# An adaLN-FFN kernel on one core: weight scales repeated by transfers instead of TensorE, the first convolution evicted by ScalarE, and a new order in front of the loop

## What is computed

```python
...
        out = lax.conv_general_dilated(x, weight, window_strides=(STRIDE,), padding=[(PAD, PAD)], dimension_numbers=('NCH', 'OIH', 'NCH'), feature_group_count=GROUPS)
        ctx = jnp.einsum('nd,od->no', c, c_weight)
        out = out + ctx[:, :, None] + bias[None, :, None]
...
        w_scale = jnp.max(jnp.abs(weight), axis=-1, keepdims=True) / QMAX
        w_q = jnp.round(weight / w_scale).astype(jnp.int8)
        a_scale = jnp.max(jnp.abs(input_act), axis=-1, keepdims=True) / QMAX
        x_q = jnp.round(input_act / a_scale).astype(jnp.int8)
        acc = jnp.matmul(x_q.astype(jnp.int32), w_q.T.astype(jnp.int32))
        scale = a_scale * w_scale.T[None, :, :]
        out = (acc.astype(jnp.float32) * scale).astype(jnp.float16)
...
    x = x + _L0_ffn_ref(_L0_cond_ref(x, cond_128, L0_cond_weight, L0_cond_c_weight, fside_S_0), L0_ffn_weight)
    x = x + _L1_ffn_ref(_L1_cond_ref(x, cond_128, L1_cond_W0, L1_cond_b0, L1_cond_W1, L1_cond_b1, L1_cond_W2, L1_cond_b2, L1_cond_weight, L1_cond_bias_k), L1_ffn_W, L1_ffn_b, L1_ffn_A, L1_ffn_Bmat, L1_ffn_LiMEs)
```

## Time and profile before

| | |
|---|---|
| runs | 612.49, 613.61, 615.41 us; median 613.61 |
| the profiled execution's own time | 613.3 us |
| its span (first to last instruction) | 611.5 us |
| granted TensorE clock | 0.999 of full speed |
| busy: PE, DVE, ACT, POOL | 604.1, 433.3, 357.0, 375.0 us |
| transfers | 136.24 MB, mean 223 GB/s |

### The profile page before, as it was taken

How to read it: one execution, slowest core, us unless ns; L and a number is a source line. 1 busy time by engine, 2 the same in 40 slices (tenths; PEclk the granted TensorE clock), 3 DMA queues, 4 the chain that set the end, 5 groups by cost and what they waited for, 6 DMA issues and landing times.

```text
span 611.5 us, 16208 instructions
## 1 busy us (share of the span) xinstructions
PE 604.1 (99%) x6500; PEld 343.7 (56%) x6500; DVE 433.3 (71%) x883; ACT 357.0 (58%) x622; POOL 375.0 (61%) x252
## 2 busy tenths in 40 slices
PE   8999999999999999999999999999999999999998
PEld 5756667667776777765554444444444444444444
DVE  5988999978899999986877757754635454355543
ACT  3799998989999999876535234453233333321100
POOL 3436545546777666554888945989777659656200
PEclk9999999999999999999999999999999999999999
DMA  8989987878889999684183125765445445542111
GB/s 338 357 268 311 366 317 277 295 261 307 318 315 333 323 336 312 232 293 140 66 305 116 34 71 201 284 234 192 159 172 185 153 169 216 207 147 94 70 69 70
DMA packets 38632, 136.24 MB, mean 223 GB/s; under 512 B 5036, under 2 KB 5580, under 8 KB 38513
## 3 DMA queue, kind: packets, MB, share of 16 engines
q1 hardware_dynamic: 33518, 118.43, 54.6%
q10 hardware_dynamic: 5040, 16.78, 6.8%
HBM read 87.95 MB, written 47.24 MB: 221 GB/s over the span
## 4 chain that ended last, share of the span: by engine, by line
PE 87%; DVE 1%; issue 1%; ACT 0%; DVEq 0%
PE ps L908 42%; PE ps L612 16%; PE ps L517 9%; PE ps L709 7%; PE ps L596 4%; PE ps L890 2%; PE ps L581 2%; PE ps L657 2%; PE ps L652 1%; PE ps L621 1%; PE ps L625 0%; PE ps L692 0%; DVE yb L1459 0%; PE ps L677 0%; ACT zT L1096 0%
## 5 line engine op out<-in xcount | busy, mean ns | idle before, releaser
L612 PE MATMUL ps<-wqT,yq_both 128*128 128x512 bf16 x512 | 122.4, 379 | 0.3 <-DVE yb L1459 0.3
L1284 POOL TENSOR_TENSOR x<-x_in,f_all 128x512 f32<-128x512 f32 x64 | 74.3, 1162 | 51.1 <-DVE f_all L1496 51.0
L1288 POOL TENSOR_TENSOR x_split<-x_ph,x_split 128x1032 f16<-128x1032 f32 x25 | 53.7, 2148 | 55.5 <-ACT x_split L994 55.5
L1021 ACT ACTIVATE yv<-yb,yinv 128x128 f32<-128x128 f32 x256 | 77.8, 388 | 0.0
L1323 POOL TENSOR_TENSOR ring<-ring 128x512 f32<-128x512 f32 x56 | 72.8, 1300 | 4.3
L612 PEld LDWEIGHTS ps<-wqT,yq_both 128*128 128x128 bf16 x512 | 45.5, 99 | 46.3 <-issue 1.4
L517 PE MATMUL ps<-x_split,conv_h 128*64 128x256 f16 (+1 forms) x1248 | 60.0, 275 | 0.0
L1496 DVE SCALAR_TENSOR_TENSOR f_all<-ps,tok_scale,wsc_b 128x512 f16<-128x512 f32 x64 | 47.9, 749 | 16.7 <-PE ps L612 15.6
L517 PEld LDWEIGHTS ps<-x_split,conv_h 128*64 128x64 f16 (+1 forms) x1248 | 47.5, 108 | 9.7 <-issue 7.9
L1817 DVE SCALAR_TENSOR_TENSOR x_in<-ps,unscale,x_in 128x512 f32<-128x512 f32 x30 | 22.5, 750 | 39.9 <-PE ps L908 39.9
L1817 DVE SCALAR_TENSOR_TENSOR wst<-ps,unscale,wst 128x512 f32<-128x512 f32 x27 | 20.2, 750 | 36.7 <-PE ps L908 36.7
(11 more groups left out here) (351 smaller groups left out, 1321.5 us busy)
## 6 DMA issues: line engine op xcount, KB each, us to landing
x_in<-in_x SPq DMA_DIRECT2D x32, 512.0 KB, 6.0
x_scratch<-x SPq DMA_DIRECT2D x32, 512.0 KB, 3.7
x_ph<-in_x_phases SPq DMA_DIRECT2D x31, 516.0 KB, 5.2
x_scratch<-ring SPq DMA_DIRECT2D x26, 512.0 KB, 5.0
ring<-x_scratch SPq DMA_DIRECT2D x26, 512.0 KB, 5.2
x_in<-x_scratch SPq DMA_DIRECT2D x12, 512.0 KB, 3.5
out<-x_in ACTq DMA_DIRECT2D x12, 512.0 KB, 3.5
wst<-in_w_rows SPq DMA_DIRECT2D x10, 512.0 KB, 6.7
```

Of the source, the lines that this page charges most:

```text
L612: last = mm(acc_bank(t, h), yqT[:, t % 2, p, :], wqT[:, p, h * HALF:(h + 1) * HALF], start=p == 0, stop=p == PH - 1)
L1021: last = A(yv[:, s, :], yb[:, t % 2, s, :], ACT.Copy, scale=yinv[:, s:s + 1], bias=MAGIC)
L1284: g.tensor_tensor(x1[:, t % 2, s], x_in[:, t % 3, s], f16[:, s], ALU.add).then_inc(sem("x1_ready"), 1)
L1288: g.tensor_tensor(x_split[:, (t - SPLIT) % 2, 1, :], phases(t), x_split[:, (t - SPLIT) % 2, 0, :], ALU.subtract).then_inc(sem("xl_ready"), 1)
```

## The change

- The matmuls that spread the scales are gone, and so are both copies to `wsc_b`. Instead ScalarE issues, per half, a transfer that writes four columns of `wq_scale` to a scratch in DRAM (`save_scales`, 128 x 4 floats, each of them by itself since the DRAM side is transposed), waits for it, and issues one that reads 512 scales back to all 128 partitions (`load_scales`). `layer0(0, h)` waits for the second. What TensorE had waited for ahead of those matmuls (`agg_ready`, `agg_b_ready`, `limesT_ready`) it now waits for at `int_product(0, h)`.
- The bias and eviction of convolution 0 go from VectorE (one instruction of 1024 columns) to ScalarE (`first_bias`, eight of 128 columns).
- What stands in front of the loop is in a new order on SP, PE, ACT and DVE. Loop step 3 is written out ahead of the loop and woven into the rest; the loop starts at 4.

```diff
+        scales_dram = nc.dram_tensor("scales_scratch", [L], F32, kind="Internal").ap()
...
             load_phases(0)
             sp.dma_start(conv_w[:, :, :], conv_taps).then_inc(sem("conv_w_loaded"), 16)
             load_wq(1)
-            sp.dma_start(pk[:, PACK_1:PACK_W], pack[:, PACK_1:PACK_W]).then_inc(sem("pack2_loaded"), 16)
+            sp.dma_start(kw, mix_rows).then_inc(sem("kw_loaded"), 16)
             load_wq(2)
-            sp.dma_start(kw, mix_rows).then_inc(sem("kw_loaded"), 16)
             load_phases(1)
             load_wq(3)
             load_wq(4)
-            load_phases(2)
             load_wq(5)
             load_wq(6)
+            sp.dma_start(pk[:, PACK_1:PACK_W], pack[:, PACK_1:PACK_W]).then_inc(sem("pack2_loaded"), 16)
+            load_phases(2)
+            load_phases(3)
+            load_phases(SPLIT)
             load_wq(7)
+            load_x(0)
             sp.dma_start(b_flat[:, :], w_b.rearrange("r (a l) -> (r a) l", a=4)).then_inc(sem("flat_loaded"), 16)
             sp.dma_start(kw_flat[:, :], mix_w.rearrange("k o i a -> (k o i a)").rearrange("(p n) -> p n", p=P)).then_inc(sem("flat_loaded"), 16)
             sp.dma_start(bias_flat[:, :], b_ffn.rearrange("(p n) -> p n", n=NL)).then_inc(sem("flat_loaded"), 16)
-            load_x(0)
-            load_phases(3)
             load_x(1)
-            load_phases(SPLIT)
             sp.dma_start(b_rank, w_b).then_inc(sem("b_loaded"), 16)
             load_x(2)
...
-            def wq_scales_out(h):
-                pe.wait_ge(sem("wq_scaled"), 8 * h + 8)
-                pe.wait_ge(sem("agg_ready"), 4)
-                if h == 0:
-                    pe.wait_ge(sem("agg_b_ready"), 1)
-                    pe.wait_ge(sem("limesT_ready"), 1)
-                for o in range(4 * h, 4 * h + 4):
-                    last = mm(ps_mix[:, o * P:(o + 1) * P], wq_scale[:, o:o + 1].to_broadcast([P, P]), ident[:, :], start=True, stop=True)
-                last.then_inc(sem("wsc_psum"), 1)
...
                         pe.wait_ge(sem("wqT_ready"), 4 * h + 4)
-                        pe.wait_ge(sem("wsc_ready"), h + 1)
+                        pe.wait_ge(sem("agg_ready"), 4)
+                        pe.wait_ge(sem("agg_b_ready"), 1)
+                        pe.wait_ge(sem("limesT_ready"), 1)
...
             wq_transposed(0)
+            agg_weights(0)
+            wq_transposed(1)
+            conv(1)
+            max_rows(0)
+            wq_transposed(2)
+            wq_transposed(3)
+            max_back(0)
+            agg_weights(1)
+            wq_transposed(4)
+            conv(2)
+            wq_transposed(5)
             pe.wait_ge(sem("pack2_loaded"), 16)
             pe.wait_ge(sem("attT_ready"), 1)
             mm(bank(2)[0:B, 256:256 + CH], attT[:, :], pk[0:NK, PACK["mixb"]], start=True, stop=True).then_inc(sem("mlp_psum"), 1)
             tr(bank(2)[0:R, 384:384 + E], pk[0:E, PACK["limes"]], ident[0:E, 0:E]).then_inc(sem("mlp_psum"), 1)
-            wq_transposed(1)
-            agg_weights(0)
-            max_rows(0)
-            conv(1)
-            max_back(0)
-            wq_transposed(2)
-            agg_weights(1)
-            wq_transposed(3)
-            conv(2)
-            wq_transposed(4)
-            wq_scales_out(0)
+            max_rows(1)
             tokens_out(0)
-            max_rows(1)
-            wq_transposed(5)
             wq_transposed(6)
-            wq_scales_out(1)
             max_back(1)
+            conv(3)
+            max_rows(2)
             wq_transposed(7)
             int_product(0, 0)
-            max_rows(2)
-            int_product(0, 1)
+            max_back(2)
             tokens_out(1)
-            max_back(2)
             pe.wait_ge(sem("s_max_ready"), 9)
             tr(ps_small[0:9, 160:288], s_max[:, :], ident[:, :]).then_inc(sem("s_top_psum"), 1)
-            conv(3)
+            int_product(0, 1)
+            pe.wait_ge(sem("s_top_ready"), 1)
+            x_total(SPLIT)
             pe.wait_ge(sem("wqT_ready"), 7)
             int_product(1, 0, 0, 4)
-            pe.wait_ge(sem("s_top_ready"), 1)
-            pe.wait_ge(sem("yinv_ready"), 3)
+            pe.wait_ge(sem("x_scale_ready"), 1)
             mm(ps_small[:, 300:309], s_top[:, 0:1].to_broadcast([9, P]), ident[0:9, 0:9], start=True, stop=True).then_inc(sem("s_top_psum"), 1)
+            int_product(1, 0, 4, 8)
+            int_product(1, 1, 0, 3)
+            pe.wait_ge(sem("s_scale_ready"), 1)
+            max_rows(3)
+            int_product(1, 1, 3, 8)
+            mix(0)
+            max_back(3)
+            tokens_out(2)
...
+            def save_scales(h):
+                act.wait_ge(sem("wq_scaled"), 8 * h + 8)
+                wait(act, "scales_saved", 16 * h)
+                o = slice(4 * h, 4 * h + 4)
+                act.dma_start(scales_dram.rearrange("(o p) -> p o", p=P)[:, o], wq_scale[:, o]).then_inc(sem("scales_saved"), 16)
+
+            def load_scales(h):
+                act.wait_ge(sem("scales_saved"), 16 * h + 16)
+                wait(act, "scales_loaded", 16 * h)
+                cols = slice(h * HALF, (h + 1) * HALF)
+                act.dma_start(wsc_b[:, cols], scales_dram[cols].rearrange("(a l) -> a l", a=1).to_broadcast([P, HALF])).then_inc(sem("scales_loaded"), 16)
+
+            def first_bias():
+                act.wait_ge(sem("conv_ready"), 1)
+                act.wait_ge(sem("att_logits_ready"), 1)
+                for n in range(8):
+                    last = A(yb[:, 0, n, :], ps_conv[:, n * MB:(n + 1) * MB], ACT.Identity, bias=ybias[:, 0, n // 2, n % 2:n % 2 + 1])
+                last.then_inc(sem("yb_ready"), 1)
...
-            act.wait_ge(sem("mlp_psum"), 5)
-            A(attT[:, :], bank(2)[0:NK, 192:192 + B], ACT.Copy).then_inc(sem("attT_ready"), 1)
-            wq_out(0)
             act.wait_ge(sem("conv_w_loaded"), 16)
             act.wait_ge(sem("s_max_zeroed"), 1)
             A(abs_junk, conv_w[:, :, :].rearrange("p g n -> p (g n)"), ACT.Abs, accum_out=s_max[:, 6:7]).then_inc(sem("s_max_ready"), 1)
+            first_bias()
+            wq_out(0)
+            wq_out(1)
+            act.wait_ge(sem("mlp_psum"), 5)
+            A(attT[:, :], bank(2)[0:NK, 192:192 + B], ACT.Copy).then_inc(sem("attT_ready"), 1)
             agg_out(0)
+            save_scales(0)
             agg_out(1)
+            wq_out(2)
+            wq_out(3)
+            load_scales(0)
+            scale_rows(0)
+            agg_out(2)
+            wq_out(4)
+            agg_out(3)
+            phase_sums(SPLIT)
+            wq_out(5)
             act.wait_ge(sem("mlp_psum"), 7)
             A(agg_b[:, :], bank(2)[0:B, 256:256 + CH], ACT.Copy).then_inc(sem("agg_b_ready"), 1)
+            tokens_sb(0)
             act.wait_ge(sem("gate_w_ready"), 1)
             A(gate_w[0:R, E:2 * E], bank(2)[0:R, 384:384 + E], ACT.Copy).then_inc(sem("limesT_ready"), 1)
-            wq_out(1)
-            wq_out(2)
-            scale_rows(0)
-            agg_out(2)
-            agg_out(3)
-            wq_out(3)
-            wq_out(4)
-            act.wait_ge(sem("wsc_psum"), 1)
-            A(wsc_b[:, 0:HALF], bank(2), ACT.Copy).then_inc(sem("wsc_ready"), 1)
-            tokens_sb(0)
-            wq_out(5)
+            save_scales(1)
+            scale_rows(1)
             wq_out(6)
+            load_scales(1)
             wq_out(7)
-            scale_rows(1)
-            phase_sums(SPLIT)
             tokens_sb(1)
-
-            for c in range(3, NT):
-                if SPLIT < c + LEAD < NT:
+            scale_rows(2)
+            act.wait_ge(sem("zeros_ready"), 1)
+            A(zT[R:64, :].rearrange("p (a e) -> p a e", e=2)[:, :, 1], z_w[R:64, 0, 0:1].to_broadcast([64 - R, NTOK // 2]), ACT.Copy).then_inc(sem("zeros_ready"), 1)
+            act.wait_ge(sem("s_scale_ready"), 2)
+            A(x_more[:, 0, :], conv_w[:, :, :].rearrange("p g n -> p (g n)"), ACT.Copy, scale=s_up[:, 6:7]).then_inc(sem("conv_h_ready"), 1)
+            act.wait_ge(sem("zeros_ready"), 2)
+            A(z_w[:, :, 0:R], pk[:, PACK["a"]].rearrange("p (k r) -> p k r", k=NL), ACT.Copy, scale=s_up[:, 1:2]).then_inc(sem("rank_hi_ready"), 1)
+            A(z_w[:, :, R:ZR], pk[:, PACK["w8"]].rearrange("p (k r) -> p k r", k=NL), ACT.Copy, scale=s_up[:, 0:1]).then_inc(sem("rank_hi_ready"), 1)
+            high(0, 0)
+            high(0, 1)
+            tokens_sb(2)
+            row_sums(0)
...
                 if t == 0:
-                    dve.wait_ge(sem("wsc_ready"), h + 1)
+                    dve.wait_ge(sem("scales_loaded"), 16 * h + 16)
...
             attention_logits()
             attention()
             wq_tile(1)
-            conv_bias(0)
             attention_sets()
+            wq_tile(2)
             row_max(0)
-            wq_tile(2)
-            chan_max(0)
             wq_tile(3)
             wq_tile(4)
+            chan_max(0)
+            conv_bias(1)
             scales(0)
-            conv_bias(1)
-            row_max(1)
```

(26 more changed lines are left out.)

33 lines of the change are left out of this document (8 added, 25 removed).

## The result

The change is **slower**: 637.51 us (median of 6 runs, 635.61 to 640.17) against 613.24 us (6 runs, 611.67 to 615.41), a ratio of 1.0398 with a 95% interval of 1.0376 to 1.0419. The profiled execution has a span of 635.4 us, before 611.5: 23.9 us more.

What follows compares the result with a forecast made beforehand. TensorE, busy 99% of the span, was taken as the bound, with ScalarE close behind. Gains of 1.90 and 0.34 us less a 0.3 us wait for the last tile gave 1.9 us: 611.7 us, range 609.6 to 616.5.

Steps and rivals of the forecast that it cites:

- Rival 1: ScalarE at `load_scales(0)`: the save lands late and the kernel is slower, 618.7 us with a 10.7 us landing; chance 0.20.
- The matmuls and the idle 0.62 us: TensorE before the loop: deleting two matmul groups wins 1.90 us, a shorter wait before tile 1's transposes 0.34 us.
- First convolution, hidden: ScalarE's eight evictions of conv(0), 2.33 us, end near 14.3 before conv(1) at 15.23; cost 0 on the path.
- The save's issue: ScalarE issues the first save near 17.1 us at 0.38 us, in time without a tile to evict.
- The save's landing: The first save lands 3 us after issue, so ScalarE does not wait at `load_scales(0)`; bounds 2.3 and 10.7 us.
- The rule that I quoted: Trainium skill on DMA: a non-contiguous last dimension makes one descriptor per element; under 64 KB a transfer is mostly overhead.
- Every microsecond beyond 3.7 reaches TensorE whole: Save landings over 3.7 us delay TensorE by the full excess, as ScalarE's chain to tile 7 has no slack.
- What costs nothing: Second save (3.3 us of cover), second load, SP's reordered transfers and the later `aggb_scratch` copy were all taken as free.
- What is won at conv(4) is won at the end: From conv(4) on TensorE's work is unedited, one string, so a lead there was taken to last to the end.

Runs made afterwards that it cites:

- experiment 10: The kernel before, old order, with only the first convolution's eviction moved from VectorE to ScalarE; 615.62 us, ratio 1.0034.
- experiment 3: The changed kernel with each save written as 128 pieces of 16 bytes instead of 512 of 4; 618.33 us, one run.
- experiment 2: The changed kernel without both saves, its loads reading a row of `w_q` and waiting for nothing; 614.74 us, one run.
- experiment 11: The changed kernel without saves, with SP's wait for agg_b and its three transfers behind the phases of tiles 4, 5 and 7; 615.24 us, ratio 1.0035.
- experiment 1: The changed kernel's order and ScalarE evictions, but scales spread by TensorE's eight matmuls and two copies as before; 613.49 us, ratio 0.9996.

## Why the prediction was wrong

It said 611.7 us, range to 616.5; the time was 637.5. Rival 1, at 0.20, was the mechanism, but its price was too low by far.

- **The matmuls and the idle 0.62 us**: right. Without saves conv(4) starts at 40.98; I had 41.3. agg_weights(0) at 13.16 (13.0), conv(1) at 15.55 (15.23).
- **First convolution, hidden**: right in this order, 12.35 to 14.5. Its price with the cover gone I had put at 2.33 us at most; experiment 10 shows 2.6 us, as the clock adds to the idle time.
- **The save's issue**: right, 0.39 us at 17.35, and ScalarE at the load near 21.2.
- **The save's landing**: this is the step that failed. I took 3 us with bounds of 2.3 and 10.7; it was 18.0 and 9.2. The low bound came from `rows_scratch`, a scatter of 4 KB that I took for "a like scatter of small pieces" without its piece size. By the kernel's text it writes 256 pieces of 16 bytes; 128 such pieces landed within 3.0 us in experiment 3. The stores that set my choice were nearly all of 512 KB, another kind of transfer (and the 1.8 us among them belongs to one of 128 KB; those of 512 KB took 2.6 at least). The upper bound was no bound: that a backlog on SP's queue made the 10.7 us said nothing of how long small writes take. The rule that I quoted named the danger (one descriptor per element) and no price.
- **Every microsecond beyond 3.7 reaches TensorE whole**: right. For landings of 6.4, 9.7 and 9.8 us the working has TensorE idle for 2.7, 6.0 and 6.1 us; the traces have 2.12, 5.70 and 5.87 before tokens_out(0). For 18.0 us it has 14.3, and there are 13.90 (1.52 before conv(2), whose phases were late, and 12.38). As a time that gives 626.0 us.
- **The rest, which I had costed at nothing.** conv(4) starts 21.8 us later than without saves. Of that, 13.90 us are the first save; 3.62 the second, behind which the last weight tile stood; 0.91 (0.30 and 0.61) follow VectorE's wait of 2.28 us for the second load; and 3.4 us are the same matmuls at a lower clock, 0.83 on average from 12 to 62.8 us.
- **"What costs nothing"**: the second save had 3.3 us of cover by my working and needed 9.2. SP's order and the aggb copy were each costed by their own cover too, and none had cover against a transfer that holds back all the others.
- **What is won at conv(4) is won at the end**: wrong as well, apart from the saves. 2.2 us were won at conv(4) and 3.5 lost in the loop. More "issue" time goes with it, in experiments 2 and 11, mostly inside strings of matmuls and just behind packets of instructions. Why there is more of it in these kernels than in the one of experiment 1, with the same order, isn't settled. Late phases alone are excluded by experiment 11, whose ten runs are 0.35% slower than the kernel before.
